# Cross-attention and a top-2 expert layer on one core: the last three batches written out per engine, the shared weights split earlier, a gather buffer per batch, and the shared tiles' x asked for sooner

## What is computed

```python
x = x + tanh(g_xattn[0]) * xattn(layernorm(x), ctx, ctx, Wq, bq, Wk, bk, Wv, bv, Wo, bo)   # 16 batches x 256 tokens x 256
x = x + tanh(g_ffn[0]) * ffn(layernorm(x), w_router, w1, w3, w2, ws1, ws3, ws2)

# xattn: 16 heads of 16, softmax(q k^T / 4) v, then Wo
# ffn, for the 4096 tokens xf:
scores = softmax(xf @ w_router)                       # 8 experts
expert_weights, expert_indices = top_k(scores, 2)
h = silu(xf @ w1[e]) * (xf @ w3[e]); y = h @ w2[e]    # hidden 512; weighted sum over the two experts = moe_out
shared = silu(xf @ ws1) * (xf @ ws3) @ ws2
out = shared / 3 + moe_out * 2 / 3
```

## Time and profile before

| what | value |
|---|---|
| median of 3 runs | 934.19 us (927.93 to 934.75) |
| the profiled execution | 931.92 us, its span 930.2 us (1.7 us lie around it) |
| PE busy | 818.6 us, 88% of the span |
| DVE, ACT, POOL busy | 535.9 (58%), 418.0 (45%), 378.9 us (41%) |
| mean granted clock of PE | 0.948 of full |

### The profile page before, as it was taken

How to read it: one execution, slowest core, us unless ns; L and a number is a source line. 1 busy time by engine, 2 the same in 40 slices (tenths; PEclk the granted TensorE clock), 3 DMA queues, 4 the chain that set the end, 5 groups by cost and what they waited for, 6 DMA issues and landing times.

```text
span 930.2 us, 19000 instructions
## 1 busy us (share of the span) xinstructions
PE 818.6 (88%) x7106; PEld 727.7 (78%) x7107; DVE 535.9 (58%) x1104; ACT 418.0 (45%) x691; POOL 378.9 (41%) x373
## 2 busy tenths in 40 slices
PE   2478999999999998878899999999999999968765
PEld 2365777677777766558799999999999999968765
DVE  4256788888888878554843444444343433535545
ACT  5228776666666655644333333333333333311211
POOL 4524446555555532325660513135051300345571
PEclk9759999999999989789999999999999999988887
DMA  4869877778888886324575413143241111234352
GB/s 147 236 129 190 202 165 209 191 189 186 206 197 191 172 172 170 132 93 164 181 250 196 133 57 124 56 124 112 69 132 60 56 57 45 86 97 129 122 153 73
DMA packets 103409, 131.47 MB, mean 141 GB/s; under 512 B 9904, under 2 KB 87472, under 8 KB 103344
## 3 DMA queue, kind: packets, MB, share of 16 engines
q1 hardware_dynamic: 91696, 93.37, 40.3%
q0 software_dynamic: 11648, 37.23, 12.1%
HBM read 75.25 MB, written 55.05 MB: 140 GB/s over the span
## 4 chain that ended last, share of the span: by engine, by line
PE 62%; DVE 18%; issue 8%; DMA 3%; ACT 3%; another core or an unknown queue 3%; SPq 1%; POOL 1%; DVEq 0%; ACTq 0%; POOLq 0%
PE bank L499 7%; PE bank L501 6%; PE bank L500 6%; DVE row_max L1178 6%; PE bank_sm L499 5%; PE bank_sm L501 5%; PE bank_sm L500 5%; PE bank_ss L499 4%; PE bank_ss L501 4%; PE bank_ss L500 4%; PE bank_sm L592 4%; PE bank_ss L581 3%; PE bank L608 3%; PE bank L517 2%
## 5 line engine op out<-in xcount | busy, mean ns | idle before, releaser
L1178 DVE TENSOR_REDUCE row_max<-bank_sm 128x4 f32<-128x1024 f32 x128 | 156.3, 1221 | 70.3 <-PE bank_sm L592 47.1
L820 ACT ACTIVATE probs_T<-bank_ss 128x1024 f32<-128x1024 f32 x128 | 131.6, 1028 | 38.7 <-PE bank_ss L581 37.3
L499 PE MATMUL bank_sm<-xg_h,w_h 128*128 128x256 f32 x400 | 119.9, 300 | 30.7 <-DVE xg_l L1052 27.6
L1052 DVE TENSOR_TENSOR gT_l<-gg,gT_h 128x1024 fp32r<-128x1024 f32 x50 | 80.8, 1616 | 95.2 <-ACT gT_h L946 90.7
L501 PE MATMUL bank_sm<-xg_l,w_h 128*128 128x256 f32 x400 | 118.6, 296 | 0.0
L500 PE MATMUL bank_sm<-xg_h,w_l 128*128 128x256 f32 x400 | 118.4, 296 | 0.0
L499 PE MATMUL bank<-w_h,gT_h 128*128 128x256 f32 x400 | 114.6, 287 | 3.2 <-DVE x_all L1289 3.2
L499 PE MATMUL bank_ss<-xg_h,w_h 128*128 128x256 f32 x400 | 116.8, 292 | 0.0
L501 PE MATMUL bank<-w_l,gT_h 128*128 128x256 f32 x400 | 114.3, 286 | 0.7 <-issue 0.7
L500 PE MATMUL bank<-w_h,gT_l 128*128 128x256 f32 x400 | 114.6, 286 | 0.4 <-issue 0.4
L500 PE MATMUL bank_ss<-xg_h,w_l 128*128 128x256 f32 x400 | 113.1, 283 | 0.0
(11 more groups left out here) (173 smaller groups left out, 2015.0 us busy)
## 6 DMA issues: line engine op xcount, KB each, us to landing
qk_d<-qk_s SPq DMA_DIRECT2D x32, 512.0 KB, 7.7
w_raw<-wall POOLq DMA_DIRECT2D x27, 512.0 KB, 3.9
k<-qk_d SPq DMA_DIRECT2D x96, 128.0 KB, 4.4
q<-qk_d SPq DMA_DIRECT2D x96, 128.0 KB, 6.4
xg<-xs_d SPq DMA_DIRECT2D x35, 256.0 KB, 2.7
ys_d<-y_s SPq DMA_DIRECT2D x34, 256.0 KB, 2.2
x<-x SPq DMA_DIRECT2D x16, 256.0 KB
c_s<-ctxT SPq DMA_DIRECT2D x16, 256.0 KB, 3.2
```

What stands on the lines that cost most here:

```text
L499: pe.matmul(out, ah, bh, start=first and k == 0, stop=False)
L820: act.activation(pT[:, 2 * (pv % 4):2 * (pv % 4) + 2, :].rearrange("p h t -> p (h t)"), SS[:, :], ACT.Exp, scale=D ** -0.5).then_inc(exp_o ...
L1052: return v.tensor_tensor(dst, ps, high.bitcast(F32), ALU.subtract)
L1178: v.tensor_reduce(mx[B.slot][:, :, :].rearrange("p t (r q) -> p r t q", r=2)[:, :, :, p], SM[:, :].rearrange("p (r t k) -> p r t k", r=2, ...
```

## The change

1. The iterations end at 15. What iterations 16 to 18 did, and the tables' pieces, stands as one written order per engine (x13, x14, x15 are the last batches). Against before, PE transposes batch 14's normed rows ahead of up1(1), and the shared work and the router's steps of the other batches are interleaved anew. POOL gives the first weights' loads ahead of everything, and splits two of three parts ahead of batch 15's scatter, the third behind it.
2. The shared weights' high part is made in iteration 13 (slots 1, 3, 5), the low part in iteration 15 (slots 0, 1, 3), x_high and x_low of tile 0 in iteration 15 (slots 1 and 2). SP asks for x of tiles 0 and 1 at the end of iteration 14 instead of 15.
3. The router's exp and its weights' scaling of batches 13 to 15 are put behind the first routed tile; `lgd` and `ex` get three buffers.
4. y_gathered has a buffer per batch (it lies over the routed weights' space), POOL gathers all 64 pieces without a wait between.
5. Mixing starts at tile 9, two batches per tile, and SP's store of a mix stands one place later against the x loads.

```diff
-            for i in range(-AHEAD, NB + 3):
+            for i in range(-AHEAD, NB):
...
         def mixed_at(j):
-            if j == NB - 1:
-                return ()
-            first = 2 * (min(j, NB - 1) - EARLY - 2)
-            return range(max(0, first), NB if j == NB else max(0, first + 2))
+            first = max(0, 2 * (min(j, NB) - EARLY - MIX_FROM))
+            return range(first, min(NB, max(0, 2 * (j + 1 - EARLY - MIX_FROM))) if j < NB else NB)
...
             for j in range(EARLY + 2, NB):
                 load_shared(j, total + (j - 1))
-                for b in mixed_at(j - 1):
+                for b in mixed_at(j - 2):
                     store_out(b)
-            for j in (NB - 1, NB):
+            for j in range(NB - 2, NB + 1):
...
+            # PE
+            scores_to_exp(x15, PAIRS - 2); values(x15, 2)
+            up1(0, SHARED)
+            scores_to_exp(x15, PAIRS - 1); logits(x13); values(x15, 3)
+            project_out(x14); rank(x13, rk_tail); attention_rows(x15)
+            up3(0, SHARED)
+            turn_out(x15); turn_norm(x14)
+            up1(1, SHARED)
+            logits(x14); project_out(x15); rank(x14, rk_tail)
+            up3(1, SHARED); down(0, SHARED)
+            turn_norm(x15)
+            up1(2, SHARED); logits(x15); up3(2, SHARED); rank(x15, rk_tail); down(1, SHARED)
...
+            # DVE
+            best_two(x13); masks(x13); residual(x14); residual_stats(x14); positions(x13, rk_tail)
+            residual_variance(x14); list_slots(x13); divide(x15); norm(x14)
+            x_low_shared(1, 1); out_low(x15); gated(0)
+            best_two(x14); masks(x14); residual(x15); residual_stats(x15); residual_variance(x15)
+            positions(x14, rk_tail); list_slots(x14)
+            g_low(0); x_low_shared(2, 2); norm(x15); gated(1); g_low(1)
+            best_two(x15); masks(x15); positions(x15, rk_tail); list_slots(x15)
+            x_low_shared(3, 3); gated(2)
...
+            # ACT
+            probs(x15, PAIRS - 2); norm_out(x13); head_out(x15, 2); probs(x15, PAIRS - 1)
+            silu(0); head_out(x15, 3); x_high_shared(1, 1); out_high(x15); norm_out(x14)
+            g_high(0); silu(1); x_high_shared(2, 2); y_early(0); norm_out(x15)
+            g_high(1); silu(2); x_high_shared(3, 3)
...
+                    if i == SPLIT_AT and p in (1, 3, 5):          # ACT, iteration 13
+                        n = p // 2
+                        act.wait_ge(w_in[n], 16)
+                        act.activation(w_h0[:, part(n)], wraw[:, part(n)], ACT.Copy).then_inc(w_used, 1)
...
+            # POOL
+            add_bias(x14); add_bias(x15)
+            for n in range(WP):
+                load_w(1, n)
+            root(x14); scatter(x13); root(x15); scatter(x14)
+            cut(1, 0, which=(0, 1)); scatter(x15); cut(1, 0, which=(2,))
...
+            carry(NB)
             for b in range(NB):
-                n = b % RG
-                moved(po, mix_ok, b - RG + 1)
-                carry(NB + b)
                 for t in range(TS):
-                    for k, dst in enumerate((yga, ygb)):
+                    for k in range(2):
```

More of the change, by code:

```diff
@@ new lines, in scores_to_exp @@
+            def scores_to_exp(V, pv):
+                if pv == 0:
+                    pe.wait_ge(mrow, V.n(32, 32))
+                moved(pe, exp_ok, V.n(PAIRS, pv))
+                for half in range(TC):
+                    for par in range(2):
+                        own = slice(ROWS * par, ROWS * par + ROWS)
+                        r = pe.matmul(SS[:, par * 512 + half * L:par * 512 + (half + 1) * L],
+                                      k4[V.slot][own, pv, half * P:(half + 1) * P], q4[V.slot][own, pv, :],
+                                      start=True, stop=True)
+                r.then_inc(ss_ps, 1)
@@ new lines, in scores_to_max @@
+            def scores_to_max(B, p):
+                if p == 0:
+                    pe.wait_ge(stk[B.slot], B.turn * 192 + 192)
+                moved(pe, mx_ok, B.n(PAIRS, p))
+                for half in range(TC):
+                    for par in range(2):
+                        own = slice(ROWS * par, ROWS * par + 3 * D)
+                        r = pe.matmul(SM[:, par * 512 + half * L:par * 512 + (half + 1) * L],
+                                      q4[B.slot][own, p, half * P:(half + 1) * P], k4[B.slot][own, p, :],
+                                      start=True, stop=True)
+                r.then_inc(sm_ps, 1)
@@ L958, in _ @@
             iterations(act, one)
+            x13, x14, x15 = (Batch(NB - k) for k in (3, 2, 1))
+            probs(x15, PAIRS - 2)
+            norm_out(x13)
+            head_out(x15, 2)
+            probs(x15, PAIRS - 1)
+            silu(0)
+            head_out(x15, 3)
+            x_high_shared(1, 1)
+            out_high(x15)
+            norm_out(x14)
+            g_high(0)
+            silu(1)
+            x_high_shared(2, 2)
+            y_early(0)
+            norm_out(x15)
+            g_high(1)
+            silu(2)
+            x_high_shared(3, 3)
             g_high(2)
@@ L1219, in _ @@
             iterations(v, one)
+            x13, x14, x15 = (Batch(NB - k) for k in (3, 2, 1))
+            best_two(x13)
+            masks(x13)
+            residual(x14)
+            residual_stats(x14)
+            positions(x13, rk_tail)
+            residual_variance(x14)
+            list_slots(x13)
+            divide(x15)
+            norm(x14)
+            x_low_shared(1, 1)
+            out_low(x15)
+            gated(0)
+            best_two(x14)
+            masks(x14)
+            residual(x15)
+            residual_stats(x15)
+            residual_variance(x15)
+            positions(x14, rk_tail)
+            list_slots(x14)
+            g_low(0)
+            x_low_shared(2, 2)
+            norm(x15)
+            gated(1)
+            g_low(1)
+            best_two(x15)
+            masks(x15)
+            positions(x15, rk_tail)
+            list_slots(x15)
+            x_low_shared(3, 3)
+            gated(2)
             v.wait_ge(cnt_ps, 1)
```

595 lines of the change are left out of this document (305 added, 290 removed).

## The result

| | median | runs |
|---|---|---|
| before | 932.29 us | 927.93 to 934.75 |
| after | 957.06 us | 953.50 to 957.66 |

The ratio is 1.0263 (95% interval 1.0212 to 1.0313): slower, where 891 was forecast. The profiled execution took 957.44 us, its span 955.7. Of all the numbers on record one fits: rival (b), span end 956.

A forecast was written before the change was run, and what follows sets the result against it. Late tiles were taken as bound by x_low's late arrival, the drain of attention by PE's waits. From the profiled 931.92 us, 33.6 and 9.0 off gave 889.3; with the median 2.3 higher, forecast 891, range 881 to 918.

The forecast's parts named there:

- rival (b): Late phase: the hold lasts as long as gathers go out; span ends at 956, time 960; chance 0.06.
- The hold: An unexplained 5.7 us delay before tile 9, after twelve back-to-back gathers; taken to come back once, no gain or loss.
- Rival (a): Late phase: the hold repeats, 5.3 times, each 5.7 us and about 1.4 for the clock: 922; chance 0.12.
- Part 1: Late shared tiles: x asked for one tile earlier, mixes from tile 9, 8.54 us per tile; 33.6 us saved.
- 13.5 - 1.4: Last tile: down(15) starts 13.5 us after up1 today, less 1.4 us for up1 at full clock.
- the ring: Gathers in three reused buffers, waiting for mixes; gathers without waits take these waits' place, by itself no gain.
- Part 2: Late phase: 64 gathers without waits take at most 86 us; 0 taken, may cost 0 to 3 us at the end.
- Part 3: Drain of attention: written-out order removes waits summing to 11.7 us, may give back 1 to 4; 9 us taken.
- the 444: Drain of attention: up1(3) was followed through all four engine orders to start at 444 us, 9.3 us earlier.
- what follows the drain moves as a whole: Behind the drain of attention: everything shifts by the drain's gain, 9 us, since PE bounds it.
- the splits in iteration 13: Attention, iteration 13: ACT's copies, 2.94 us in three pieces, fall between exps; 0 to 1 us lost, 0 taken.
- The lock: Drain: POOL and two-input DVE operations lock each other out, 2.4 us at most per hit; 0 taken, range 0 to 4.

The follow-up runs named there:

- plain: The changed kernel with 64 plain DMAs of the same size and queue in place of the gathers; 885.45 us.
- small: The changed kernel with each gather taking only 64 of the 256 columns, a quarter of the bytes; 951.77 us.
- land2: The changed kernel with POOL waiting after every eight gathers until they have landed, about 2 us; 901.56 us, ratio 0.9703 to before.
- again_land2: land2 unedited, run once more on a chip that shows the hold; 904.52 us, ratio 0.9744 to before.
- land4: The changed kernel with POOL waiting after every sixteen gathers until they have landed, about 2 us; 944.83 us, ratio 1.0154 to before.
- nomiddle: The kernel before with parts 1 and 2 and the short breaks of mid8, without part 3; 889.78 us, ratio 0.9800 to before.
- mid8: The changed kernel with four of POOL's small additions after every eight gathers, no wait for landing; 887.36 us, ratio 0.9771 to before.
- p1only: The kernel before with part 1 alone: x loaded two tiles ahead, mixes from tile 9; 933.97 us, ratio 1.0023 to before.
- p2only: The kernel before with part 2 alone: a gather buffer per batch, 64 gathers without waits; 983.72 us, ratio 1.0584 to before.
- mid8tab: mid8 with gated(3) and tile 4's low x amid DVE's table operations; 879.75 us (0.9670), on a chip with the hold 944.97 (1.0137).
- land1: The changed kernel with POOL waiting after every four gathers until they have landed, about 2 us; 916.25 us, ratio 0.9848 to before.
- ring3: The changed kernel with the old wait restored: gathers of batch b wait until batch b-3 is mixed; 922.43 us, ratio 0.9911 to before.

## Why the prediction was wrong

**The step that failed** is "The hold": "I take it to come back once: no gain, no loss", with 0.06 for rival (b). It lasts as long as gathers go out, and 8 us more. It costs 957 - 885 = 72 us (after against plain, where the same bytes move without a hold, beside 932 and 931 for before; small against plain, within one call, 66). Rival (b) ended the span at 956, the forecast at 887.6, 68 us apart. That (b) came out to the microsecond is partly luck: it had the hold end 1.7 us behind a row that ends at 880, measured are 8 us behind one that ends at 876, and it let PE stand still before up1(9), while PE crept through up1 and up3 of tile 9. I had the row for it: the earlier trace rows, one wait of 7.50 us with no known releaser at the end of the only row of twelve gathers. What I held against it was that rows of eight show nothing of this size. That was no evidence: ACT's longest wait with an unnamed releaser grows with the row, 1.9 us behind four scatters (before), 4.3 and 5.5 in rows of eight (land2, again_land2), 7.5 behind twelve, 17.7 in rows of sixteen (land4), 39.3 in the row of 64. In before the late x may hide what rows of eight do. And the waits behind the scatters of attention, nineteen in the same trace, were overlooked: the wait behind twelve was one of a kind, not an exception. A row of 12 is also the longest in before, and the change made it 64; the one number for which the trace had no case was the one I priced at today's value. Rival (a), each twelve costs 5.7, is wrong too: it has the hold end and begin anew, and a row that isn't broken has one hold.

**Part 1, -33.6.** Right where there is no hold: 8.54 us per tile in the changed kernel behind 889.78, in nomiddle and in mid8, no wait for xg_l. down(15) waits for x_all as before, 3.22 us, in PE's timeline of after:

```profile
932.49 0.28 PE L504 MATMUL bank_sm<-xg_h,w_h 128*128 128x256 f32 x1
944.40 0.55 PE L504 MATMUL bank<-w_h,gT_h 128*128 128x256 f32 x1 [3.22 <-DVE x_all L1390]
```

It starts 11.9 us behind up1(15), as 13.5 - 1.4 said (12.1), and 11.3 us later the span ends (11.4). But p1only shows that the term can't be had by itself on a chip with the hold (1.0023): faster mixes free the ring's buffers faster, and the gathers' rows grow. I had counted the ring only as a wait; it was the brake that kept most rows at eight.

**Part 2, 0, at most 3.** It costs 5.8% alone (p2only). The 86 us for 64 gathers were right (82), and the place of the ring's wait was taken by the hold. The two steps interact: the gathers' rows are set by part 2 or, in the ring, by part 1's denser mixes.

**Part 3, -9.0.** The traces of the two profiles stand 9.1 us apart at up1(7) (789.96 against 799.08), but the terms are others. up1(3) came at 436.99, 7 us ahead of the 444 that I had followed through the orders, and 16.2 ahead of before; then 5.64 us went into the wait for xg_l before up1(4), which I didn't have: "what follows the drain moves as a whole" was wrong. 3.6 of the 5.64 us are the lock (below), most of the rest is that the table begins 3.4 us behind up1(3) where it began 1.6 behind it.

That two profiles stand 9.1 apart where I forecast 9 is luck, since attention itself varies by several us between profiles. Counted from the last row maximum of attention, the first sg of up1(4) comes after 84.1 to 87.9 us with the old order (before, p1only, p2only, nomiddle) and after 76.6 to 82.5 with the new one in thirteen profiles; the means are 86.3 and 79.5. At up1(7) they are 419.7 and 412.3, 7.4 us apart. What lies ahead of the last row maximum goes against this: iterations 13 and 14, from batch 13's last row maximum to batch 15's, take 41.7 us in the mean with the old order and 44.8 with the new one on the chips with the hold, 36.6 (one profile) and 38.3 on the others. So the splits in iteration 13, priced at 0 to 1 us, seem to cost 2 to 3; no run has them alone. That leaves 4 to 5 us for part 3. The whole kernels, mid8 against nomiddle, differ by 2.4 us, their spans by 3.9. The gathers' end sets the end in both, but it hides nothing, since the gathers begin when the middle is over (781.81 and 785.76). So 9 was about twice what the runs support. Cutting the table in two brings the sg of up1(4) to 70.8 to 71.5, some 8 us sooner, and mid8tab 7.6 us below mid8, more than the wait I aimed at; on the chip with the hold it gains nothing (944.96 and 944.97).

The sums have two small slips: up1(3) at 444 is 9.2 us earlier, not 9.3, and 889.3 + 2.3 is 891.6, not 891. Neither matters here.

**The lock.** POOL's subtraction of 2.37 us and DVE's operation of 2.36 us begin together, as the rows above show. The Trainium skill (SBUF — State Buffer, Who interferes with whom) has an operation of DVE that needs the port pair shared with GpSimd, and one of GpSimd, lock each other out for a whole instruction, and the trace agrees. Four of DVE's small operations between 430 and 446 us take 1.63 to 2.36 us where such take 0.2, and each ends within 0.05 us of the end of one of POOL's (431.77, 436.20, 443.68 and 446.14 against 431.74, 436.17, 443.64 and 446.10). The prediction spoke of operations with two inputs only; three of these four have one. The two in the table are 3.6 us of the lateness of xg_l. I had allowed 0 to 4 us and taken 0; that term of the sum measured 3.6.

**What is shown and what isn't.** Shown: the gathers hold PE (land1, land2, plain against after); neither bytes nor the queue do it (small, plain); on a chip with the hold, rows of four with 2 us between leave PE free in the late phase, rows of eight with 2 us between leave waits for its signals of up to 5.5 us at little cost in time, and rows of eight with 1.2 us between and of sixteen with 2 us hold it. The mean rate alone doesn't decide: ring3 has one gather per 1.94 us and is held in its rows of sixteen, again_land2 has one per 1.59 and keeps its time. Not shown: by which path an indirect DMA of POOL reaches PE (whether PE waits for instructions, for one, is open; the DMA view of after shows no packet of the instruction queues between 806 and 884 us, which speaks neither way); whether a pause must last until the landing or some length is enough; what differs in the chips; whether 64 in a row hold PE on a chip of the second kind.

## What to carry to other kernels

A wait that you take away may have been the brake on a burst; ask not only what the freed engine does sooner but how long it then works without a pause, and look in the trace for what happened at the longest such stretch so far. An unexplained wait at the extreme of a quantity that the change multiplies is the first thing to price, not a rarity; list all waits with an unnamed releaser in the trace, small ones too, and see what stands beside each. Indirect DMAs in long rows wanted a pause until the last had landed here, after at most eight, and a kernel with such rows has to be timed on more than one chip.

## What the runs showed of the hardware that wasn't expected

- A row of POOL's indirect DMAs, one each 1.26 us, stops PE from about 12 us into the row (after): a matmul each 2.1 to 2.8 us, semaphores up to 52 us behind the last recorded matmul, free again 8 us behind the row. The row of 64 costs 66 to 72 us.
- Short rows show it too: beside four scatters ACT waits 1.0 to 1.9 us for PE (before), where a chip of the other kind has no such wait (nomiddle), and in rows of eight up to 5.5 (again_land2).
- 64 plain DMAs of the same queue, one each 0.53 us, with the same 8 MB, do nothing to PE. An indirect one of a quarter of the bytes is issued in the same 0.96 us and holds PE as much.
- The chips differ: the same program took 879.8 us on one and 945.0 on another (mid8tab), beside 912.8 and 935.0 for the kernel before.
- Small DVE operations with a single input wait for POOL's too: 1.63 to 2.36 us for 8 columns or fewer, where such take 0.2 (after).
